# Stages without emptied seams, and the short slots' value products of a causal attention taken in pairs

## The reference

```
x = x + memory(xn) + ffn0(xn)        # layer 0
x = x + attn1(xn)  + moe1(xn)        # layer 1
memory: 8 chunks of 64 positions; each takes a gradient step of a small MLP, then the queries go through it
ffn0:   conv3 -> attention (16 heads of 8, no mask) -> layer norm -> softmax mixture of 8 experts (128-512-128) -> layer norm
attn1:  causal attention (16 heads of 8) -> conv3 -> new queries -> causal attention with the same k, v -> out
moe1:   top 8 of 32 experts, 128 slots each, silu(gate)*up, down, weighted sum back
```

## Time and profile before

| | before |
|---|---|
| median of 3 runs | 3641.94 us (3640.04 to 3645.77) |
| the profiled execution | 3637.72 us |
| its span, first to last instruction | 3635.9 us |
| PE busy | 3242.8 us (89%) |
| DVE busy | 2579.5 us (71%) |
| ACT busy | 2060.6 us (57%) |
| POOL busy | 838.3 us (23%) |
| mean granted TensorE clock | 0.958 |

### The profile page before, as it was taken

The page is one execution under the profiler, slowest core; times in us unless marked ns, Lnnn a source line. Parts: engine busy times, 40 slices in busy tenths (PEclk is TensorE's granted clock), DMA queues, the critical chain, the costliest instruction groups (busy, mean ns, idle before and its releaser), DMA issues. The chain is left out here.

```text
span 3635.9 us, 77371 instructions
## 1 busy us (share of the span) xinstructions
PE 3242.8 (89%) x30347; PEld 1888.3 (52%) x30347; DVE 2579.5 (71%) x5080; ACT 2060.6 (57%) x4148; POOL 838.3 (23%) x752
## 2 busy tenths in 40 slices
PE   6877599999999699999999999649999999999998
PEld 5776222222222277777777777425555545454454
DVE  5776588888888256776766767457777777777774
ACT  5664077777777444434334434116667776777666
POOL 3321211101110132423324224133332112111100
PEclk8998699999999799999999999769999999999999
DMA  4100111111110000110110100132221121111201
GB/s 125 30 13 1 54 51 51 39 54 51 48 51 28 27 24 22 32 34 22 33 33 28 35 25 23 37 84 60 61 59 39 46 58 50 48 45 42 55 26 29
DMA packets 180545, 151.95 MB, mean 42 GB/s; under 512 B 44396, under 2 KB 160972, under 8 KB 180044
## 3 DMA queue, kind: packets, MB, share of 16 engines
q1 hardware_dynamic: 174028, 142.07, 14.0%
q0 software_dynamic: 6144, 4.72, 0.9%
HBM read 48.45 MB, written 32.65 MB: 22 GB/s over the span
## 5 line engine op out<-in xcount | busy, mean ns | idle before, releaser
L1323 DVE TENSOR_REDUCE b_maxima<-psum 128x2 f32<-128x1024 f32 (+3 forms) x768 | 774.1, 1044 | 263.8 <-PE psum L1175 231.0
L1281 ACT ACTIVATE b_prob<-psum 128x512 f32<-128x512 f32 (+2 forms) x1536 | 725.4, 526 | 342.1 <-PE psum L1208 311.3
L1323 DVE TENSOR_REDUCE c_maxima<-psum 128x2 f32<-128x1024 f32 x512 | 602.5, 1220 | 132.4 <-PE psum L1169 131.3
L1281 ACT ACTIVATE c_prob<-psum 128x512 f32<-128x512 f32 x1024 | 535.8, 602 | 186.4 <-PE psum L1201 186.4
L1785 PEld LDWEIGHTS psum<-consts_layer,a_hid 128*128 128x128 f32 x4096 | 476.2, 192 | 53.6 <-issue 53.3
L1785 PE MATMUL psum<-consts_layer,a_hid 128*128 128x128 f32 x4096 | 477.8, 274 | 0.0
L1775 PE MATMUL psum<-a_x1t,consts_layer 128*128 128x512 f32 x1024 | 461.0, 595 | 9.4 <-issue 9.1
L1842 ACT ACTIVATE a_hid<-psum,consts_layer 128x512 f32<-128x512 f32 x512 | 346.8, 687 | 203.1 <-PE psum L1775 196.2
L1201 PE MATMUL psum<-b_qa,b_ka 64*128 64x512 bf16 (+3 forms) x2048 | 364.2, 303 | 64.2 <-ACT b_prob L1281 61.6
L1223 PE MATMUL psum<-b_prob,b_v 128*32 128x512 f32 (+3 forms) x4096 | 384.7, 448 | 0.3
L1169 PE MATMUL psum<-b_ka,b_qa 62*128 62x512 bf16 (+3 forms) x2048 | 299.5, 306 | 47.2 <-DMA b_ka<-b_part 29.7
(11 more groups left out here) (332 smaller groups left out, 4298.1 us busy)
## 6 DMA issues: line engine op xcount, KB each, us to landing
b_qa<-b_part SPq DMA_DIRECT2D x192, 128.0 KB
c_qa<-c_part SPq DMA_DIRECT2D x96, 128.0 KB, 2.5
c_ka<-c_part SPq DMA_DIRECT2D x96, 128.0 KB, 2.5
b_ka<-b_part SPq DMA_DIRECT2D x96, 128.0 KB
consts_layer<-layer_in SPq DMA_DIRECT2D x1, 5419.0 KB, 19.1
m_xin<-x SPq DMA_DIRECT2D x16, 256.0 KB, 3.8
xnt<-m_xt SPq DMA_DIRECT2D x16, 256.0 KB, 2.9
c_xt<-xnt SPq DMA_DIRECT2D x16, 256.0 KB, 2.7
```

The source lines that it names most:

```text
L1281: self.nc.scalar.activation(out, src, ACT.Exp, scale=SCALE).then_inc(self.s.free, 1)
L1323: self.nc.vector.reduce_max(out, src, X).then_inc(self.m.free, 1)
```

## The change

It has six parts.

1. The blocks between the stages go. `learn`'s semaphores are cleared by SP at the end of `attend0`, behind its last store; those of the other stages are not cleared. The constants of layer 1 have memory of their own and are loaded in `learn`, right behind those of layer 0. PE waits for the constants of its stage in its own stream.
2. Buffers of rows are cleared and given their fixed rows one by one, in the order of the turns that use them first (`fresh`): the two of turn 0 before all else, the others on DVE behind `vector_first`. `sync_fresh` copies cover and ones just before a turn's `sync_rows`. The cover's table holds the first row of ones as well, so one transfer for ones goes.
3. The parts of turn 0 are made on DVE (`vector_first`), not on POOL, and their six key rows are issued from ACT's queue (`scalar_rows`).
4. POOL makes the covers first and then clears `v` buffer by buffer; DVE's values wait for their own buffer. The experts' tables come after these.
5. `total`, `excl` and the counts move from turn -2 (slots 1, 2, 3) to turn -1 (slots 9, 10, 11), and `FIRST_GROUP` from -1 to 0, so that each finding and passing comes a turn later; the parked outputs move with them.
6. In the causal attention the values' product of t = 2 is no longer made in slot 3 but in the next slot 0, just before that of t = 3. The exponentials of t = 3 go to the free first 128 columns of the buffer that holds those of t = 2, and slot 0's exponentials wait only for the product of t = 1.

```diff
-                for sem in self.made:
-                    sp.sem_clear(sem)
+    def clear(self, sp):
+        for sem in self.made:
+            sp.sem_clear(sem)
...
+        self.fresh = []
+        for p, turn in enumerate(turns):
+            if p < BUFFERS:
+                self.fresh.append((p, "queries", self.qa[p]))
+            if turn.first and turn.batch < n_keys:
+                self.fresh.append((p, "keys", self.ka[turn.batch]))
...
+    def valued(self, s):
+        if not self.causal:
+            return [s - 1]
+        return {0: [s - 2, s - 1], T - 1: []}.get(s % T, [s - 1])
+
+    def probabilities(self, s):
+        q0 = s % T * P if self.causal else 0
+        if not self.causal:
+            return s % 2, q0
+        g, t = divmod(s, T)
+        return (g + (t == 1)) % 2, 0 if t == T - 1 else q0
...
+    def sync_fresh(self, sp, p):
+        for n, (turn, kind, x) in enumerate(self.fresh):
+            if turn != p:
+                continue
+            sp.wait_ge(self.rows_cleared, n + 1)
+            if self.causal:
+                sp.wait_ge(self.covers_ready, 5)
+                cover = self.covers[:, int(kind == "keys")].rearrange("r t p -> r (t p)")
+                sp.dma_start(x[PARTS::PITCH, :, :], cover...).then_inc(self.fresh_loaded[p], 16)
+            if kind == "keys":
+                sp.wait_ge(self.tables_ready, 1)
+                for w in range(int(self.causal), 2):
+                    sp.dma_start(x[SHIFT + w::HALF, :, :], self.one...).then_inc(self.fresh_loaded[p], 16)
...
     def sync_rows(self, sp, p):
+        self.sync_fresh(sp, p)
         sp.wait_ge(self.parted, 4 * p + 4)
         for r in range(PARTS):
...
-                                    self.prob[:, s % 2, j, q0:S], start=..., stop=...)
+                                    self.prob[:, n, j, c0:c0 + S - q0], start=..., stop=...)
...
-            if s and self.has(p):
-                self.tensor_values(pe, p, s - 1)
-            if s == 0 and self.has(p - 1):
-                self.tensor_values(pe, p - 1, SLOTS - 1)
+            for k in self.valued(s):
+                if self.has(p if k >= 0 else p - 1):
+                    self.tensor_values(pe, p if k >= 0 else p - 1, k % SLOTS)
...
         if u == 0 and p * SLOTS + s >= 2:
-            act.wait_ge(self.pv_ready, p * SLOTS + s - 1)
+            act.wait_ge(self.pv_ready, p * SLOTS + s - (2 if self.causal and s % T == 0 else 1))
...
+    def vector_clear(self, buffers):
+        for _, _, x in buffers:
+            self.nc.vector.memset(x[:, :, :], 0.0).then_inc(self.rows_cleared, 1)
+
+    def vector_first(self, dve, ready):
+        dve.wait_ge(self.s.free, ready)
+        nc.vector.tensor_copy(self.part[0][:, :, :], self.qk[:, :, :]).then_inc(self.parted, 1)
+        dve.wait_ge(self.parted, 1)
+        nc.vector.tensor_tensor(self.rest..., self.qk..., self.part[0]..., ALU.subtract).then_inc(self.parted, 1)
+        dve.wait_ge(self.parted, 2)
+        nc.vector.tensor_copy(self.part[1]..., self.rest...).then_inc(self.parted, 1)
+        dve.wait_ge(self.parted, 3)
+        nc.vector.tensor_tensor(self.part[2]..., self.rest..., self.part[1]..., ALU.subtract).then_inc(self.parted, 1)
+        self.vector_clear(self.fresh[self.cleared(0):])
...
-    TOTAL, BEFORE, UPTO = 1, 2, 3
+    TOTAL, BEFORE, INCLUDED = 9, 10, 11
...
-FIRST_GROUP = -1
+FIRST_GROUP = 0
...
-                p = whole_turn + 1 - whole_turn % 2 + 2 * b
+                p = whole_turn + 1 + whole_turn % 2 + 2 * b
...
-            with nc.Block() as block:
-                @block.sync
-                def _(sp):
-                    sp.dma_start(consts["layer1"][:, :], given["layer1"]).then_inc(loaded, 16)
-                    sp.wait_ge(loaded, 48)
...
+                    sp.dma_start(consts["layer1"][:, :], given["layer1"]).then_inc(loaded1, 16)
+                learned = first.enter_context(Semaphores())
+                learn(nc, learned, K, ps, bank, x, xnt_d, mem, memw1t, loaded, load_consts, load_layer0)
+            attend0(nc, ctx, K, ps, bank, loaded0, learned, xnt_d, xc_d, ctxt_d)
+            learned.close()
```

More of the change, by code:

```diff
@@ L1031, in loads, with cleared, prepared @@
         return sum(PARTS * (1 + u.first) for u in self.turns[:p + 1])
+    def cleared(self, p):
+        return sum(turn <= p for turn, _, _ in self.fresh)
+    def prepared(self, p):
+        return sum((kind == "keys") + 1 if self.causal else 2 * (kind == "keys") for turn, kind, _ in self.fresh if turn == p)
     def together(self, s):
@@ L1142, in sync_rows @@
-            if self.turns[p].first:
-                sp.dma_start(self.keys(p)[r::PITCH, :, :], self.part[K_PARTS[r]][:, 1, :]).then_inc(self.rows_loaded, 16)
+            self.query_row(sp, p, r)
+            if self.turns[p].first and p:
+                self.key_row(sp, p, r)
     def sync_shift(self, sp, p, n):
         groups = slice(0, 2 * EARLY) if n == 0 else slice(2 * EARLY, 2 * G)
+        if p < BUFFERS and self.causal:
+            sp.wait_ge(self.fresh_loaded[p], 16 * self.prepared(p))
@@ L1287, in scalar_context, with scalar_rows @@
         self.nc.scalar.activation(self.c[pair % 2][:, :], self.acc, ACT.Copy).then_inc(self.c_copied, 1)
+    def scalar_rows(self, act):
+        act.wait_ge(self.rows_cleared, self.cleared(0))
+        act.wait_ge(self.parted, 4)
+        for r in range(PARTS):
+            self.key_row(act, 0, r)
     def scalar_turn(self, act, p, whole, extra):
@@ L1372, with attend0 @@
     first: bool
-def attend0(nc, ctx0, K, ps, bank, xnt_d, xc_d, ctxt_d):
+def attend0(nc, ctx0, K, ps, bank, consts_loaded, learned, xnt_d, xc_d, ctxt_d):
     with ExitStack() as ctx:
@@ L1517, in extra @@
                 def extra(p, s):
+                    if s == VALUES and p == -2:
+                        att.vector_first(dve, att.s.count("k", 0))
                     if s == VALUES and att.has(p + 2):
-                        if p + 2 == 0:
-                            dve.wait_ge(att.values_cleared, 2)
                         att.vector_values(dve, p + 2, K("vbias0"))
-                att.vector_setup(dve)
+                att.vector_clear(att.fresh[:att.cleared(0)])
                 for p in range(-2, NB + 1):
@@ L2285, with layer1 @@
     parked: bool
[L2288 removed]
+def layer1(nc, ctx0, K, ps, bank, consts_loaded, chosen, gate_up, down, xnt2_d, table_d, sum_d, result):
     with ExitStack() as ctx:
```

132 lines of the change are left out of this document (58 added, 74 removed).

## The result

The changed kernel takes 3612.8 us (median of 4, 3610.9 to 3615.1) beside 3641.1 for the kernel before: ratio 0.992, 95% interval 0.9907 to 0.9932. That is 28.3 us less, where I forecast 39.9. The profiled execution's span went from 3635.9 to 3608.9 us.

| stretch | saved, us | forecast |
|---|---|---|
| `learn` (one load more, else unchanged) | 1.2 | - |
| first seam, up to the start of `attend0` | 4.8 | 3.8 |
| start of `attend0` to its first maximum | 2.3 | 4.1 |
| rest of `attend0` | -0.1 | 0 |
| second seam | -0.6 | 0.5 |

What follows compares the result with a forecast made beforehand. No single bound: PE in plain turns, DVE in turn -1, nothing busy at the seams. Terms 3.8 + 4.1 + 0.5 + 7.0 + 18.5 + 5.5 - 3.5 + 4 = 39.9 us saved, giving 3602 us; range 3590 to 3614 (8 in 10: 3584 to 3626).

Steps and rivals of the forecast that it cites:

- the pairs' term: Values' products in `layer1`: plain groups lose 0.08 us, groups where ACT ends last gain 0.12; 4 us saved over 32 turns.
- Block ends and clears, 3.8 and 7.0 us: Block ends and semaphore clears removed: 3.8 us saved in the first seam, 7.0 in the last, up to `layer1`'s start.
- Second seam, +0.5: Before `mixture`: a block end and 20 clears go, `learn`'s 58 clears run beside the landing and outlast it; 0.5 us saved.
- Start of `attend0`, 4.1: Start to first maximum: parts made on DVE, rows issued on two queues, DVE's clears end last at 24.4 us; 4.1 saved.
- Start of `layer1`, 18.5: Start to first maximum: k's copy earlier, parts on DVE, rows sooner, 1.5 us allowed for POOL delaying DVE; 18.5 saved.
- Rival D: Last seam: both of DVE's casts wait for POOL and the clears follow; 2 us worse, 3604 us; chance 0.35.
- Turn -1, 5.5: First 12 slots of `layer1`'s turn -1: finding and waiting go, `total`'s products and `excl` come in; 5.5 us saved.
- The finding in turn 7, 3.5, and the passing, free: `layer1`: the finding returns in turn 7, 3.5 us lost; the passing leaving turn 0 returns in turn 8 at the same price.
- rival B: Pairs cost 0.08 to 0.2 us per group, also where ACT was thought last: 10 to 26 us, 3616 to 3632; chance 0.12.

Runs made afterwards that it cites:

- experiment 9: Changed kernel with `learn`'s 58 semaphores cleared by SP in turn 2 of the first attention, not behind its last store; 3611.7 us beside 3641.9 for the kernel before.
- experiment 5: Changed kernel with turn 0's six key-row transfers back on SP's queue behind the query rows; 3616.3 us (1 run) beside 3641.9 for the kernel before.
- Experiment 7: The mended `total` kernel: changed kernel with `total`, `excl` in turn -2, POOL's routing tables first, ACT's key rows issued before copying `total`; 3585.3 us, kernel before 3619.9.
- experiment 10: Changed kernel without pairs, t = 3's product before slot 0's second scores unit, `learn`'s clears early, `total` in turn -2 as mended; 3576.2 us, kernel before 3619.9.
- experiment 8: First finding back in turn -1: on the changed kernel with unmended `total` in turn -2, 3619.3 us (before: 3641.9); on experiment 10's kernel, 3579.6 (before: 3619.9).
- experiment 2: Two runs: changed kernel without the pairs, 3607.4 us; kernel before with the pairs alone, 3643.9 us; the kernel before took 3636.5.
- Experiment 4: Changed kernel with the pair of values' products between the first and second unit of slot 0's scores, not behind both; 3573.6 us beside 3619.9 for the kernel before.
- value or pair first: Changed kernel with t = 3's product (single products, 3600.8 us, before 3636.5) or the pair (3573.6, before 3619.9) ahead of slot 0's second scores unit.

## Why the prediction was right, and where it was wrong

The time lies in the range and the sign is right; the size came out 11.6 us too large. With the pairs' term wrong in its sign, the time lies only 1.2 us inside the range's upper edge, so that it lies inside at all is partly luck. The sum also has a slip: by its own prices, +0.08 us for a plain group and -0.12 for the others, the pairs come to 2.5 x (-0.12) + 1.5 x 0.08 = -0.18 per turn, 5.8 us in all and not 4, since I put the pair's saving of 0.12 where the group's 0.08 belonged. With them the forecast would have been 41.7 us, still further off. Step by step:

- **Block ends and clears, 3.8 and 7.0 us:** 4.8 and 7.6. The direction was right. I charged a block end 1.2 us and more; with the semaphores' clears gone it costs 0.28 us at most in the first seam.
- **Second seam, +0.5:** -0.6. The sign failed. "They run beside the landing and are longer than it" was right, and by more than I took: 1.9 us (experiment 9).
- **Start of `attend0`, 4.1:** 2.3. The failed step is "about half of the issuing goes, some 4 us": from the first issue to the first product it is 9.9 us with two queues and 9.5 with one (experiment 5). So the rows, and not DVE's clears, end last. The parts were ready 15.7 us behind the start, 0.6 later than forecast, and the rows came 9.9 us behind them and not 6.5 to 7.
- **Start of `layer1`, 18.5:** 20.7. Most of the difference is the 1.5 us that I took for POOL holding up DVE. Rival D did not come in the changed kernel: DVE's first cast started 0.03 us after k was ready and took 0.83 us, 0.69 in `attend0`. But that is luck of the timing, since POOL's clear of the first `v` had ended 0.13 us before k was ready. In the kernels of experiments 7 and 10 k came during that clear: DVE's cast started 0.35 to 0.45 us before the clear's end and took 0.90 and 1.00 us. So a clear does lengthen a cast that starts beside it, here by 0.2 to 0.3 us; what it costs when more of the clear is left no run shows. In the changed kernel POOL paid: `qmask` took 1.25 us and 0.23 before the change. By the Trainium skill ("SBUF — State Buffer", section "SBUF: two separate sides"), the one of the two that starts first keeps the shared ports for its whole instruction and the other waits. The rows agree: DVE's subtraction ran from 2344.87 to 2346.10, and `qmask`, started 0.06 us behind it, ended at 2346.18.
- **Turn -1, 5.5:** 1.8. "two maxima ahead of DVE cover some 2" of `total`'s 3.68 us failed: DVE waited 2.86 us. Experiment 7 gets 3.1 us of it back.
- **The finding in turn 7, 3.5, and the passing, free:** 4.6 and 3.0 in the first pair of traces, but these turns also hold waits that the trace puts down to nothing on the core (below). Without such waits 1.1 and 2.8 (experiment 8). The sum was near, the split was not.
- **The pairs, +4:** -5.5 to -7.4 (experiment 2), between the forecast and rival B (a cost of 10 us and more). At 9.5 of the 11.6 us it is the step that decided the error. The plain group was priced right in kind: the new wait for the bank was there (the second product starts 0.46 us behind the first; 0.4 taken), and the pair saved 0.15 (0.12 taken). But it lost 0.20 us and not 0.08, because ACT started 0.16 later than I took. What failed is "ACT ... chain ends last. It starts up to 0.38 earlier, and PE's longer tail hides behind it": the other three groups in four show +0.01 to +0.02 us each (55.30 - 55.22 over six) instead of the -0.12 that I gave five of the six. In a group with a convolution, slot 0's second unit stands behind PE's own products, so that PE sets the time there too:

```profile
3150.02 0.44 PE L1244 MATMUL psum<-b_qa,b_ka 64*128 64x512 bf16 x2
...
3150.78 1.56 PE L2514 MATMUL psum<-b_cpad,consts_layer 128*128 128x256 f32 x6
3152.27 0.39 PE L1244 MATMUL psum<-b_qa,b_ka 64*128 64x512 bf16 x2
3152.65 0.86 PE L1267 MATMUL psum<-b_prob,b_v 128*32 128x256 f32 x16
```

  With the maxima's products between the first two, PE has no gap here. I had named the engine by which extra work a slot has, and had not walked one such group as I had walked the plain one. The groups with q, k or the context's copy are not walked here either.
- Experiment 4 shows the cause: not the pair, but its place behind the second unit, whose last product waits for a bank while the pair could run.

## What to carry to other kernels

Work that is taken out of one place must be put where it fills a wait that is there: the same pair cost 0.5 us per two turns behind the second unit and gained 0.5 in front of it. Before a transfer's issues are spread over queues, compare first issue to landing with the sum of the issues; where the transfers land no faster than one queue issues them, a second queue brings nothing. When a job is moved into idle time, walk all that it waits for on every engine and all that is queued behind it, small tables and DMA issues included.

## What the runs showed of the hardware that I had not expected

**Waits put down to nothing on the core.** The waits from slot 12 of turn -1 to the end of turn 8 that the trace puts down to "remote", in the kernel before:

```profile
DVE b_maxima L1323 <- remote: 23.7, 7, 4.6
ACT b_prob L1281 <- remote: 18.2, 4, 9.2
```

41.9 us in all, part of it on both engines at the same time; 28.1 in the changed kernel, 18 to 30 in the other runs of the first three sets, and none in the four profiles of the last set, where the kernel before takes 3619.9 and not 3636 to 3642 us. The stretch from slot 12 of turn -1 to turn 9, the same code in both, takes 398.9 us in the changed kernel and 370.8 in the mended `total` kernel of the last set: 28.1 us less, as much as the waits. So part of the difference between two traces in turns 0 to 8 is theirs and not the change's. It touches the main number too: the mended `total` kernel saved 34.6 us where these waits are absent, of which 2.7 are its own, so the changed kernel would save some 32 there (an estimate), nearer to the forecast than 28.3. What the waits are stays open. That the chips differ is not shown: the set with 3641.9 us for the kernel before and the set with 3619.9 bear the same chip number.

**The clock in the last turn.** The last turn, where PE has no maxima to make, ran at full clock before (38.3 us). In some runs the clock fell to half within it: without the pairs the turn took 42.4 us, 4.1 more, at a mean of 0.83.

```profile
3561.37:3603.80 42.43, 32.63 (x352) 15.15 (x351) 4.29 (x10) 23.93 (x51) 2.55 (x2) 0.83 0.09 26
3581.37:3585.37 4.00, 4.00 (x29) 0.95 (x28) 0.78 (x2) 1.09 (x2) 0.00 (x0) 0.50 0.00 0
```

At 0.50, 1.2 GHz, the eight values' products of 512 columns took 1.94 us instead of 1.06. From 10 to 2 us before it fell PE was busy 3.66 and 3.41 of each 4 us, as in the kernel before, where it stayed up (3.67 and 3.38). In the runs with value or pair first it fell as well (40.7 to 42.9 us), so 2 to 5 us of what they gain in the turns is not in their time. Why it falls in some kernels and stays up in others is open.
